# Two chunks of a SiLU gate computed from tanh on ScalarE and two products on VectorE, in the second sweep of a two-layer kernel

## The reference, cut to what matters

```
# encoder's feed-forward
h = jax.nn.elu(out1 @ W1 + b1)
ffn_out = h @ W2 + b2
# mixture of experts, 16 experts of 64 hidden features, and the shared expert of 256
shared = jnp.einsum('bls,ds->bld', jax.nn.silu(jnp.einsum('bld,sd->bls', x, sfc1)) * jnp.einsum('bld,sd->bls', x, sfc2), sfc3)
h = jax.nn.silu(jnp.einsum('td,ehd->teh', xf, w1))
moe = jnp.einsum('teh,te,edh->td', h, dispatch, w2)
```

## Time and profile before

| | |
|---|---|
| median of 3 runs | 3318.87 us (3318.83 to 3323.17) |
| the profiled execution | 3322.94 us, span 3321.1 us |
| PE busy | 2789.5 us, 84% |
| DVE busy | 2613.0 us, 79% |
| ACT busy | 2363.8 us, 71% |
| second sweep | from about 2072 us to the end; a full step takes 73.87 us |

### The profile page before, as it was taken

How to read it: one execution, slowest core, us unless ns; L and a number is a source line. 1 busy time by engine, 2 the same in 40 slices (tenths; PEclk the granted TensorE clock), 3 DMA queues, 4 the chain that set the end, 5 groups by cost and what they waited for, 6 DMA issues and landing times. The chain is left out here.

```text
span 3321.1 us, 53374 instructions
## 1 busy us (share of the span) xinstructions
PE 2789.5 (84%) x15818; PEld 2094.3 (63%) x15818; DVE 2613.0 (79%) x4418; ACT 2363.8 (71%) x5178; POOL 1012.2 (30%) x683
## 2 busy tenths in 40 slices
PE   3487898898888888888888897789998889899986
PEld 1164665565565566566556664577887778778875
DVE  4999999999999999999999952566666666666663
ACT  4466686777767768667676754468888888888873
POOL 1544344344444434434434310011111111111111
PEclk6588999999999999999999899999999999999999
DMA  2000000000000000000000002000000000000000
GB/s 112 8 4 15 18 4 21 17 11 13 17 21 3 21 17 3 21 17 3 21 17 14 4 18 79 15 15 19 28 17 17 25 17 17 17 17 28 17 9 15
DMA packets 49779, 64.41 MB, mean 19 GB/s; under 512 B 3584, under 2 KB 36416, under 8 KB 49184
## 3 DMA queue, kind: packets, MB, share of 16 engines
q1 hardware_dynamic: 47392, 54.93, 5.0%
q10 hardware_dynamic: 2304, 8.46, 0.6%
HBM read 41.78 MB, written 21.60 MB: 19 GB/s over the span
## 5 line engine op out<-in xcount | busy, mean ns | idle before, releaser
L800 POOL TENSOR_TENSOR acc<-acc,shared 128x1024 f32<-128x1024 f32 x256 | 610.8, 2386 | 881.5 <-DVE shared L1127 805.5
L1127 DVE TENSOR_TENSOR_SCAN shared<-shared 128x1024 f32<-128x1024 f32 x256 | 600.1, 2344 | 16.6 <-issue 7.1
L944 PEld LDWEIGHTS bank<-one_sb,hid 128*128 128x128 f32 x4096 | 479.6, 193 | 30.4 <-issue 17.2
L944 PE MATMUL bank<-one_sb,hid 128*128 128x128 f32 x4096 | 482.1, 276 | 14.5 <-ACT hid L663 14.5
L163 POOL TENSOR_SCALAR n_ve<-n_mv 128x4 f32<-128x4 f32 x96 | 58.1, 605 | 1141.9 <-DVE n_mv L141 1141.9
L891 PE MATMUL bank<-S,pick_sb 96*128 96x512 bf16 x512 | 211.0, 418 | 229.6 <-DVE shared L1139 117.4
L631 ACT ACTIVATE shared<-shared,aneg 128x512 f32<-128x512 f32 (+1 forms) x512 | 341.3, 723 | 62.3 <-DVE shared L1127 46.7
L1139 DVE TENSOR_TENSOR shared<-shared,bank 128x1024 f32<-128x1024 f32 x256 | 312.5, 1221 | 15.5 <-POOL acc L800 4.5
L891 PEld LDWEIGHTS bank<-S,pick_sb 96*128 96x128 bf16 x512 | 50.5, 99 | 425.5 <-DVE shared L1139 178.7
L1120 DVE TENSOR_TENSOR shared<-shared,bank 128x1024 f32<-128x1024 f32 x256 | 309.2, 1208 | 0.4 <-PE bank L891 0.3
L663 ACT ACTIVATE hid<-banks,one_sb 128x512 f32<-128x512 f32 x304 | 208.7, 692 | 110.5 <-PE bank L944 67.3
(11 more groups left out here) (275 smaller groups left out, 7056.9 us busy)
## 6 DMA issues: line engine op xcount, KB each, us to landing
kv_dram<-Gs ACTq DMA_DIRECT2D x16, 516.5 KB, 3.1
kvl<-kv_dram SPq DMA_DIRECT2D x16, 516.5 KB, 3.7
xs<-in_x SPq DMA_DIRECT2D x16, 256.0 KB, 2.9
x<-in_x SPq DMA_DIRECT2D x16, 256.0 KB, 2.9
x_dram<-x SPq DMA_DIRECT2D x16, 256.0 KB, 2.1
h_dram<-hT SPq DMA_DIRECT2D x16, 256.0 KB, 2.0
h<-h_dram SPq DMA_DIRECT2D x16, 256.0 KB, 2.6
x2s<-x_dram SPq DMA_DIRECT2D x16, 256.0 KB, 2.6
```

The costliest lines, as they stand in the source:

```text
L800: pool.tensor_tensor(acc[:, :, :], acc[:, :, :], zz[:, k % 2, :, :], ALU.add)\
L944: last = pe.matmul(bank1(f"down{e}")[:, j * D:(j + 1) * D], hid[:, e % 2, f, j * P:(j + 1) * P], w2[:, e, f, :], start=(f == 0), stop=(f = ...
L1127: dve.tensor_tensor_scan(h[:, :, :].rearrange("p g t -> p (g t)"), dec[:, k % 2, :, :].rearrange("p g t -> p (g t)"), u[:, :, :].rearrange ...
```

## The change

For chunks 1 and 2 ACT computes `th = tanh(x/2)` into a new buffer. DVE then computes `sl = (th + 1) * x`, which increments `sl_ok`, and `hm = (sl * 0.5) * y`, as silu(x) = x (1 + tanh(x/2)) / 2. Both are scalar_tensor_tensor ops. Chunks 0 and 3 to 9 stay as they are.

```diff
         NX = MC + SC
+        th = sb("th", [P, 2, T])
         sl = sb("sl", [P, 2, T])
...
+        BY_TANH = (1, 2)
...
                 def silu(q, d):
                     act.wait_ge(*xps(d, q + 1))
                     act.wait_ge(*hm_ok(d, q - 1 if q >= 2 else 0))
+                    if q in BY_TANH:
+                        act.activation(th[:, q % 2, :], bankD(f"x{q}")[:, :], ACT.Tanh, scale=0.5)\
+                           .then_inc(th_ok.sem, 1)
+                        return
                     act.activation(sl[:, q % 2, :], bankD(f"x{q}")[:, :], ACT.Silu).then_inc(sl_ok.sem, 1)
...
                 def chunk(q, d):
 
+                    if q in BY_TANH:
+                        dve.wait_ge(*th_ok(d, BY_TANH.index(q) + 1))
+                        dve.wait_ge(*hm_ok(d, q - 1 if q >= 2 else 0))
+                        dve.scalar_tensor_tensor(sl[:, q % 2, :], th[:, q % 2, :], 1.0, bankD(f"x{q}")[:, :],
+                                                 ALU.add, ALU.mult).then_inc(sl_ok.sem, 1)
                     dve.wait_ge(*sl_ok(d, q + 1))
                     dve.wait_ge(*yps(d, q + 1))
                     if q == 0:
                         dve.wait_ge(*mo(d, 0))
+                    if q in BY_TANH:
+                        dve.scalar_tensor_tensor(hm[:, q, :], sl[:, q % 2, :], 0.5, bankD(f"y{q}")[:, :],
+                                                 ALU.mult, ALU.mult).then_inc(hm_ok.sem, 1)
+                        return
                     dve.tensor_tensor(hm[:, q, :], sl[:, q % 2, :], bankD(f"y{q}")[:, :], ALU.mult)\
                         .then_inc(hm_ok.sem, 1)
```

More of the change, by code:

```diff
@@ L1413, in sweep_two @@
         (w1ps, vb_ok, ee_ok, he, w2ps, gg_ok, t6a, t6b, x3_ok, x3_kept, lg_ok, gidx, gd_ok, gex_ok, disp_ok, dtp, dT_ok,
-         xps, yps, sl_ok, hm_ok, mo, fin, ob_ok, chainD) = (sig(n, p) for n, p in (
+         xps, yps, th_ok, sl_ok, hm_ok, mo, fin, ob_ok, chainD) = (sig(n, p) for n, p in (
              ("w1ps", FC), ("vb_ok", FC), ("ee_ok", FC), ("he", FC), ("w2ps", 1), ("gg_ok", 1), ("t6a", 1),
              ("t6b", 1), ("x3_ok", 1), ("x3_kept", 1), ("lg_ok", 1), ("gidx", 1), ("gd_ok", 1), ("gex_ok", 1), ("disp_ok", 1),
-             ("dtp", 1), ("dT_ok", 1), ("xps", NX), ("yps", NX), ("sl_ok", NX), ("hm_ok", NX),
+             ("dtp", 1), ("dT_ok", 1), ("xps", NX), ("yps", NX), ("th_ok", 2), ("sl_ok", NX), ("hm_ok", NX),
              ("mo", 1), ("fin", 1), ("ob_ok", 1), ("chainD", 8)))
```

## The result

Measured in turns with the kernel before on one chip, the changed kernel took 3332.13 us (median of 9, 3326.41 to 3335.32) against 3320.93 (median of 9). The ratio is 1.0032, interval 1.0023 to 1.0041: slower, by more than the 0.2% that this kernel's measurement can tell. The forecast was 3323.1, which is within 0.2%; its range ended at 3332. It started from a median of 3318.87 for the kernel before; the measured ratio on that is 3329.5, inside the range.

The account below looks back on a forecast made before the run. DVE and PE releasing each other, not ACT, were taken to bound slots 2 and 3. 14 full steps of 0.3 us, 4.2 us, with the steps without attention cancelling, took the median from 3318.87 to 3323.1 us; range 3311 to 3332.

Parts of the forecast that it names:

- the chain of a full step: Slots 2 to 5: `w0` waits for the new DVE op, later work follows late; a full step 0.3 us longer.
- part (1): Four table loads removed from slots 2 and 3: worth 0.27 us a step in slot 2, nothing in slot 3.
- part (3): One more 0.69 us DVE op per chunk ahead of `sl_ok`: `w0` 0.53 to 0.61 us late, slot 5 0.20 to 0.36.
- 14 full steps of 0.3 us: Second sweep: all 14 full steps lose 0.3 us each, 4.2 us together, 2.8 to 5.0 from the handoffs.
- the 6.6 that it called the bound: Whole kernel: 0.2%, 6.6 us, is what a measurement can tell from no change.
- Steps without attention: Steps 16 and 17: about 1.4 us gained in step 16 and 1.4 us lost in step 17, which cancel.
- A: Rival, slots 2 and 3: the loads were the bound; up to 2.1 us a step gained, 3289 us; chance 0.13.
- B: Rival, slot 2: the DVE op is free and 0.27 us a step stays as gain, 3315 us; chance 0.12.
- C: Rival, `w0` and `w2`: PE's delay reaches the next slot in full, 0.6 to 0.8 us a step, 3327 to 3330; chance 0.25.

Follow-up runs that it names:

- chunk1: Tanh and two products for chunk 1 only, chunk 2 by SiLU, against the kernel before: full step 74.13 us, median 0.10% slower.
- chunk2: Tanh and two products for chunk 2 only, chunk 1 by SiLU, against the kernel before: full step 73.85 us, median 0.03% slower.
- dup_front: The changed kernel with chunk 1's product computed once more into a spare buffer ahead of the real one on DVE: full step 74.73 us.
- dup_back: The changed kernel with a spare DVE op of the product's size behind `hm` of chunk 1: full step 74.13 us.
- loadsback: The changed kernel with a one-element SiLU ahead of each tanh, which brings the table loads back: full step 74.22 us.
- tanhonly: The kernel before with tanh for SiLU in chunks 1 and 2, products on DVE left out: full step 73.36 us.

## Why the prediction was right or wrong

**Right: the chain of a full step.** Taken was 0.3 us a step, measured 0.27. `w0` +0.53 (forecast 0.53 to 0.61), `vb` and the square of slot 3 +0.27 (0.26 to 0.34), L1806 +0.27 (0.26 to 0.34), `qm` +0.26 (0.20 to 0.36); `w2` +0.45, just under 0.46 to 0.62. The product took 679 ns where 0.69 was taken, the tanh 593 ns where 0.58 to 0.60 was; ACT waits 1.79 us ahead of the exp where 1.6 was forecast. The loads of the second sweep are 199 for 257 (the whole kernel has 329 for 387). chunk1, chunk2, dup_front and dup_back show that the cause is the one named, and a full step of 74.13 lies in the forecast 74.1 to 74.2.

**Right in sum, wrong in two terms: part (1), "nothing in slot 3", and part (3).** Without the product the step is 0.51 us shorter, not 0.27: the square of slot 4 did wait for ACT, contrary to "ACT is not late: it could begin the square of slot 4 before 2524.75". And measured from there the product costs 0.77, not 0.57. The two errors, of 0.24 and 0.20, all but cancel, because the product's delay of PE covers nearly all that the loads of slot 3 had held up; with the product in place, loadsback shows 0.09 for all four loads. Anyone who had used part (1) to price the loads alone would have been wrong by half.

**What a load costs ACT.** Square and the next op start 0.48 us apart without a load between them (2507.50 to 2507.98), and 1.89 with one (2507.33 to 2509.22). That is 1.41 us for 1283 ns of load, so 0.13 beyond it, where part (1) said that no further drain was seen. The Trainium skill's figure for a switch (same page, section "What ACT_TABLE_LOAD costs") is 2.66 us; the trace does not agree.

**The step that failed: the sum, "14 full steps of 0.3 us".** It holds for the thirteen steps 2 to 14: 3.64 us measured, where 13 times 0.3 is 3.9. The fourteenth, step 15, lost 3.43: 0.27 by the chain and 3.16 by DVE's stall and PE's halved clock behind it (chunk1, whose stall stands off the path, lost 0.35 there). The prediction looked at one step of the middle and took the last to be like it, though its code is written out once behind the loop; it had no term for instructions that come late there. This term alone takes the forecast of +4.2 to +7.4, past the 6.6 that it called the bound. With the stall moved away by a pad the kernel measures +4.79 us (3324.35 less 3319.56) and +4.55 (3325.02 less 3320.47), which is the forecast's size. That moving the stall takes the loss from 0.32% to 0.15% is shown by two pads, and all thirteen traces show the instruction packets beside it.

**Steps without attention** were to cancel. From the last `o1T` to the end the changed kernel took 1.05 us more in this pair of profiles, but that stretch lasted 81.77 and 82.99 us in two kernels with the old chunks and 81.51 to 86.83 in six with both new ones. The granted clock differs in it (windows of the changed kernel, then of before):

```profile
3265.00:3295.00 30.00, 21.58 (x113) 17.40 (x112) 12.51 (x53) 7.44 (x12) 5.07 (x6) 0.79 0.00 1
```

```profile
3260.00:3290.00 30.00, 20.15 (x120) 16.52 (x120) 12.44 (x53) 7.44 (x12) 5.08 (x6) 0.90 0.00 1
```

So the term is not confirmed, and a microsecond or two of loss may lie there. The difference of the medians is 11.2 us; 7.1 are in the spans, the rest in that both profiles lie some 2 us off their medians in opposite directions. Of the 11.2, 3.9 are the chain, 3.2 step 15, and about 4 are not assigned.

**The rivals.** A is refuted by tanhonly (0.51 for 2.1 us a step) and loadsback, B by dup_front. C gave the right sign and nearly the right time by another way: its price was 0.47 us a step and more, and no step of the loop paid it. The range reached up to 3332 on C's account alone, so that the result comes out at its edge, and not far outside, is luck.

## What to carry to other kernels

A table load is worth what the engine behind it waits for, and an op put in its place costs what stands behind *it*: read both from the timeline, slot by slot (here -1.11 us a step in one slot, +0.27 in another, from the same edit). Where an engine waits for the signal that frees a PSUM bank and nothing behind it has slack, work put ahead of the signal is passed on in full (0.60 of 0.60 us in slot 2), and the same work behind the signal is free. And when the expected effect is some tenths of a per cent, look at the code that runs once behind a loop by itself, look at what a wait with no releaser has beside it among the instruction packets, and time the change with the program padded by a few instructions too.

## What the runs showed of the hardware

- Behind the 12 turns of the loop, in which no instruction packet was moved on queue 14, two of 8 KB come 2.4 to 2.7 us apart, in all thirteen kernels. DVE stood still beside the first of such a pair, for 1.45 to 2.62 us with no releaser in the ten kernels with the product, and went on 1.70 to 1.94 us after its start. Where DVE was waiting for ACT anyway (4.21 and 3.89 us), nothing shows. On the path, 2.17 us of it cost 3.16, with PE's halved clock behind it.
- PE, at 2.4 GHz before, had the granted clock at 0.50 (1.2 GHz) from 3180 to 3184 us, behind an idle time of 3.54 us, and back at 1.00 by 3188. In the full step shown, where its longest wait in slot 2 is 1.19 us, it stays at 1.00.
- A tanh needs no load beside an exp: none is placed between the square, the tanh and the exp of slots 2 and 3.
